# First projection of three batches moved into the first attention, in half units

## What is computed

```
qkv = x @ qkv_w.T                              # q, k, v of 16 heads
scores = alpha * tanh(q @ k.T / beta)
f, g: tanh(x @ [hex_w, q6_w].T), 12 values per token
scores += (f mixed by a 12x12 table per head) @ g.T
attn = softmax(causal(scores)); out = (attn @ v) @ out_w.T
```

## Time and profile before

| | |
|---|---|
| median of 3 runs | 4458.54 us (4456.73 to 4461.19) |
| the profiled execution's own time | 4471.63 us |
| span in its profile | 4469.8 us |
| busy share of the span | PE 86%, ACT 77%, DVE 64%, POOL 10% |
| mean granted clock of TensorE | 0.959 |
| tanh of layer 0's attention (L775), busy in all | 1102.9 us, 640 instructions |
| exp of layer 0's attention (L785) | 1065.6 us, 640 instructions |
| sums of layer 0's attention (L835) | 1569.5 us, 2560 instructions |

### The profile page before, as it was taken

The page is one execution under the profiler, slowest core; times in us unless marked ns, Lnnn a source line. Parts: engine busy times, 40 slices in busy tenths (PEclk is TensorE's granted clock), DMA queues, the critical chain, the costliest instruction groups (busy, mean ns, idle before and its releaser), DMA issues. The chain is left out here.

```text
span 4469.8 us, 66988 instructions
## 1 busy us (share of the span) xinstructions
PE 3854.6 (86%) x21966; PEld 1406.6 (31%) x21966; DVE 2840.0 (64%) x5324; ACT 3432.6 (77%) x3144; POOL 450.8 (10%) x407
## 2 busy tenths in 40 slices
PE   6958888888888888888888776758999999999787
PEld 2422222222222222222222463432222222222465
DVE  5637777777777777777777796872233332332588
ACT  2429999999999999999999412337999999999333
POOL 3520000000000000000000124650000000000133
PEclk9979999999999999999999888988999999999899
DMA  5851111112111112111111345562222222222332
GB/s 174 260 175 53 48 52 39 42 48 57 43 52 42 42 49 56 44 50 41 39 56 30 115 141 155 169 187 77 72 73 60 79 66 71 75 58 65 98 92 85
DMA packets 307816, 360.48 MB, mean 81 GB/s; under 512 B 56590, under 2 KB 237934, under 8 KB 307249
## 3 DMA queue, kind: packets, MB, share of 16 engines
q1 hardware_dynamic: 307508, 356.62, 27.4%
HBM read 228.15 MB, written 128.25 MB: 80 GB/s over the span
## 5 line engine op out<-in xcount | busy, mean ns | idle before, releaser
L835 DVE SCALAR_TENSOR_TENSOR att_prob<-att_tanh,alpha,ps 128x512 f32<-128x512 f32 (+3 forms) x2560 | 1569.5, 661 | 525.4 <-ACT att_tanh L775 333.9
L716 PE MATMUL ps<-att_q,att_k 99*128 99x512 bf16 (+7 forms) x5120 | 1196.7, 355 | 173.6 <-DMA att_v<-v_ones 79.1
L743 PE MATMUL ps<-att_prob,att_v 128*32 128x512 f32 (+3 forms) x10240 | 1215.1, 547 | 10.2 <-ACT att_prob L785 5.3
L775 ACT ACTIVATE att_tanh<-ps,rbeta 128x2048 f32<-128x2048 f32 (+3 forms) x640 | 1102.9, 1723 | 123.3 <-PE ps L716 123.3
L781 ACT ACTIVATE att_prob<-ps 128x1024 f32<-128x1024 f32 (+3 forms) x1280 | 1051.9, 920 | 78.4 <-PE ps L716 70.1
L785 ACT ACTIVATE att_prob<-att_prob 128x2048 f32<-128x2048 f32 (+3 forms) x640 | 1065.6, 1665 | 52.1 <-DVE att_prob L835 49.6
L725 PE MATMUL ps<-att_f,att_g 75*128 75x512 bf16 (+3 forms) x2560 | 854.0, 361 | 177.9 <-DVE att_prob L835 153.3
L716 PEld LDWEIGHTS ps<-att_q,att_k 96*128 96x128 bf16 (+1 forms) x5120 | 396.8, 99 | 1045.4 <-ACT att_prob L781 430.4
L823 DVE TENSOR_TENSOR att_prob<-att_prob,keep 128x256 f32<-128x256 f32 x512 | 211.5, 423 | 647.3 <-ACT att_prob L781 642.2
L725 PEld LDWEIGHTS ps<-att_f,att_g 75*128 75x128 bf16 x2560 | 235.7, 97 | 1060.8 <-DVE att_prob L835 1029.1
L743 PEld LDWEIGHTS ps<-att_prob,att_v 128*32 128x32 f32 x10240 | 202.5, 108 | 391.8 <-issue 147.2
(11 more groups left out here) (132 smaller groups left out, 2470.9 us busy)
## 6 DMA issues: line engine op xcount, KB each, us to landing
att_k<-k_parts SPq DMA_DIRECT2D x768, 64.0 KB
att_q<-q_parts SPq DMA_DIRECT2D x768, 64.0 KB
v_ones<-proj_vs SPq DMA_DIRECT2D x128, 256.0 KB, 3.1
att_v<-v_ones SPq DMA_DIRECT2D x128, 256.0 KB
post_o<-o_t SPq DMA_DIRECT2D x40, 512.0 KB, 5.1
att_f<-f_parts SPq DMA_DIRECT2D x384, 48.0 KB
o_t<-att_on SPq DMA_DIRECT2D x512, 32.0 KB, 1.9
q_parts<-proj_parts SPq DMA_DIRECT2D x32, 384.0 KB, 4.1
```

The source lines that it names most:

```text
L716: mm = pe.matmul(ps[:, bank, off:TG], keys, q_s[:, n % QU, h, off:TG], start=True, stop=True)
L743: mm = pe.matmul(ps[VW * h:VW * (h + 1), O0 + n % 2, off:TG], v_s[:, c % KU, kb % CB, h * VW:(h + 1) * VW], prob[:, S % R, h, off:TG], sta ...
L775: th.done(act.activation(tanh_s[:, S % 2, :, off:TG], ps[:, QK0:QK0 + HQ, off:TG], ACT.Tanh, scale=kn["rbeta"][:, 0:1]))
L835: sc.done(dve.scalar_tensor_tensor(prob[:, S % R, h, off:TG], tanh_s[:, S % 2, h, off:TG], kn["alpha"][:, 0:1], ps[:, E0 + h % 2, off:TG], ...
```

## The change

Layer 0's projection phase now handles batch 0 alone (`NB=1`). The projection of batches 1 to 3 (12 groups) is done inside the attention of the batch before it. A group has 9 units there: g, q0, q1, k0, k1, f0, f1, v0, v1; each unit but the two f is cut in two halves, so there are 16 halves per group, 64 per batch and 192 in all. One half is issued at the end of every second step of PE, in steps 2, 4, ... 128 of a batch's 160. Halves of g, q and k are one of the two 128-channel products of a tile; a half of v is one of two blocks of 128 tokens. The products gather in PSUM bank 7.

- That bank is taken from the outputs: `OU = 1`, so the first `weigh` of a group waits for the transpose of the group just before. This first `weigh` (the "late" one) is issued at the end of its PE step, behind `extra(S, 3)` and ahead of the half, in all 16 sets.
- DVE copies each finished unit except g out of PSUM (8 per group, 96 in all) between the second and third sum of the next step. `normalise` moves from there to the front of the step's sums.
- ACT makes g with one tanh of 12 x 512 per group, ahead of its exp.
- POOL, idle in attention until now, does the whole split: four operations per tile, 84 tiles.
- SP loads four weights and two groups of x behind the first of its loads, stores 7 tiles and 2 x 4 pieces of v per group and loads x further on, in turns with the attention's loads, five steps behind PE. The loads of a new batch wait until its projection is stored.
- `row_max_phase` gets the projection too, in its skipped body.

```
-    QK0, E0, O0 = 0, 4, 6
+    QK0, E0, O0, BG = 0, 4, 6, 7
+    OU = 1 if layer == 0 else 2
+    kinds = tiles + [("v", 0), ("v", 1)]
+    NU = len(kinds)
+    N_UNIT = (B - 1) * GB * NU if layer == 0 else 0
+    EVERY = 2
+    halves = [(gq * NU + u, half) for gq in range(GB) for u, (kind, _) in enumerate(kinds) for half in range(1 if kind == "f" else 2)]
+    def half_at(S):
+        b, s = divmod(S, NHQ * NST)
+        i, rest = divmod(s - 2, EVERY)
+        if not N_UNIT or b == B - 1 or rest or not 0 <= i < len(halves):
+            return None
+        return b * (GB * NU) + halves[i][0], halves[i][1]
...
         def _(sp):
...
+            def store_unit(j):
+                X, kind, m, tile, n = unit(j)
+                b, gq = X // GB + 1, X % GB
+                if kind == "v":
+                    bg_ev.wait(sp, j)
...
+                    if m == 1 and X + 2 < N_UNIT // NU:
+                        load_x(X + 2)
+                else:
+                    low.wait(sp, tile)
...
+                    parts_out.done(sp.dma_start(kn[f"{kind}_d"][:, row:row + n, :].rearrange("k r t -> r k t"), parts[0:n, tile % 2]), tile % 2)
...
+            for n in range(QU):
+                load(n)
+                if layer == 0 and n == 0:
+                    for name, t in (("wq", wq_s), ("wk", wk_s), ("wv", wv_s), ("w12", w12_s)):
+                        sp.dma_start(t[:], w[name]).then_inc(w_in, 16)
+                    load_x(0)
+                    load_x(1)
+            LATE = LAG + 3
+            for S in range(LATE, N + LATE):
...
+                if last:
+                    if n + QU < NG:
+                        o_tr.wait(sp, n)
+                        b = (n + QU) // (GB * NHQ)
+                        if layer == 0 and b > 0 and (n + QU) // GB % NHQ == 0:
+                            projected((b - 1) * GB + (n + QU) % GB)
+                        load(n + QU)
+                    store_o(n)
+                if unit_at(S - LATE) is not None:
+                    store_unit(unit_at(S - LATE))
...
         def _(pe):
+            def project(j, half):
+                X, kind, m, tile, n = unit(j)
+                if half == 0:
...
+                    bg_ev.wait(pe, j - 1)
+                if kind == "f":
+                    mm = pe.matmul(ps[0:n, BG], kn["Cq"][:].rearrange("p q e h -> p (q e h)")[:, m * n:(m + 1) * n], f12[:, X % 2], start=True, stop=True)
+                elif kind == "v":
+                    at_t = slice((2 * m + half) * P, (2 * m + half + 1) * P)
+                    for c in range(DC):
+                        mm = pe.matmul(ps[:, BG, half * D:(half + 1) * D], xt_s[:, X % 2, c, at_t], wv_s[:, c, :], start=c == 0, stop=c == DC - 1)
+                else:
+                    lhs = w12_s[:, half, :] if kind == "g" else (wq_s if kind == "q" else wk_s)[:, half, m * P:(m + 1) * P]
+                    mm = pe.matmul(ps[0:n, BG], lhs, xt_s[:, X % 2, half], start=half == 0, stop=half == 1)
+                if half == 1 or kind == "f":
+                    bg_ps.done(mm)
...
-                    o_tr.wait(pe, n - 2)
+                    o_tr.wait(pe, n - OU)
...
-                if S >= LAG:
+                late = layer == 0 and S >= LAG and at(S - LAG)[2] == 0
+                if S >= LAG and not late:
                     weigh(S - LAG)
...
                     extra(S, 3)
+                if layer == 0 and late:
+                    weigh(S - LAG)
+                if half_at(S):
+                    project(*half_at(S))
...
         def _(act):
+            def feature(j):
+                X, kind, m, tile, n = unit(j)
+                if kind == "g":
+                    bg_ps.wait(act, j)
...
+                    bg_ev.done(act.activation(f12[:, X % 2], ps[0:NF, BG], ACT.Tanh))
...
+                if S > 0 and unit_at(S - 1) is not None:
+                    feature(unit_at(S - 1))
                 if S > 0 and layer == 0:
...
         def _(dve):
+            if layer == 0:
+                dve.memset(vs[:], 1.0).then_inc(ones_set, 1)
...
+            def evict(j):
+                X, kind, m, tile, n = unit(j)
+                if kind == "v":
...
+                    bg_ev.done(dve.tensor_copy(vs[:, m, :, :, 0:HD], ps[:, BG].rearrange("p (t h d) -> p t h d", t=2, h=H)))
+                elif kind != "g":
+                    bg_ps.wait(dve, j)
+                    low.wait(dve, tile - 2)
+                    bg_ev.done(dve.tensor_copy(raw[0:n, tile % 2], ps[0:n, BG]))
...
-                        o_tr.done(dve.transpose(ot_s[:, v].rearrange("p b n -> p (b n)"), ps[:, O0 + v]))
+                        o_tr.done(dve.transpose(ot_s[:, v].rearrange("p b n -> p (b n)"), ps[:, O0 + G % OU]))
...
                 for h in range(HQ):
-                    if h == 2:
+                    if h == 0:
                         normalise(due, 2 if g <= 1 else 1)
+                    if h == 2 and S > 0 and unit_at(S - 1) is not None:
+                        evict(unit_at(S - 1))
...
+            @block.gpsimd
+            def _(pool):
...
+                    bg_ev.wait(pool, j)
+                    parts_out.wait(pool, u, tile // 2 - 1)
+                    hi.done(pool.tensor_copy(parts[0:n, u, 0], src))
...
+                    rest.done(pool.tensor_tensor(rem[0:n], src, parts[0:n, u, 0], ALU.subtract))
...
+                    mid.done(pool.tensor_copy(parts[0:n, u, 1], rem[0:n]))
...
+                    low.done(pool.tensor_tensor(parts[0:n, u, 2], rem[0:n], parts[0:n, u, 1], ALU.subtract))
...
-        project_phase(nc, kn, 0, {"wq": chunked(a["wq0"]), "wk": chunked(a["wk0"]), "wv": chunked(a["wv0"]), "w12": chunked(a["w12"]), "xt": chunked(a["x0_t"])}, None)
-        row_max_phase(nc, kn, 0)
-        attend_phase(nc, kn, 0)
+        project_phase(nc, kn, 0, w0, None, NB=1)
+        row_max_phase(nc, kn, 0, w0)
+        attend_phase(nc, kn, 0, w0)
```

More of the change, by code:

```diff
@@ L683, in _ @@
                 sp.dma_start(k_s[QROWS:QROWS + 3], kn["ones_d"][:, 0:KU * HQ * TG].rearrange("p (u h t) -> p u h t", u=KU, h=HQ)).then_inc(ones_in, 16)
[L684 to L694, removed]
+            for n in range(QU):
[7 more added lines that the diff above has]
+            for S in range(LATE, N + LATE):
+                it, g, *_, last = at(S - LATE)
+                n = it * GB + g
+                if last:
[8 more added lines that the diff above has]
+                    store_unit(unit_at(S - LATE))
             for u in range(2):
@@ L767, in _ @@
                 c.start(act)
+            def feature(j):
+                X, kind, m, tile, n = unit(j)
+                if kind == "g":
+                    bg_ps.wait(act, j)
+                    if X >= 2:
+                        low.wait(act, tile - 2 * NTL)
+                    bg_ev.done(act.activation(f12[:, X % 2], ps[0:NF, BG], ACT.Tanh))
             for S in range(N + 1):
@@ L848, in _, with row_max_phase @@
             assert not due
-def row_max_phase(nc, kn, layer):
+        if layer == 0:
+            @block.gpsimd
+            def _(pool):
+                for c in (hi, rest, mid, low):
+                    c.start(pool)
+                for j in range(N_UNIT):
+                    X, kind, m, tile, n = unit(j)
+                    if kind == "v":
+                        continue
+                    u = tile % 2
+                    src = f12[:, X % 2] if kind == "g" else raw[0:n, u]
+                    bg_ev.wait(pool, j)
+                    parts_out.wait(pool, u, tile // 2 - 1)
+                    hi.done(pool.tensor_copy(parts[0:n, u, 0], src))
+                    hi.wait(pool, tile)
+                    low.wait(pool, tile - 1)
+                    rest.done(pool.tensor_tensor(rem[0:n], src, parts[0:n, u, 0], ALU.subtract))
+                    rest.wait(pool, tile)
+                    mid.done(pool.tensor_copy(parts[0:n, u, 1], rem[0:n]))
+                    mid.wait(pool, tile)
+                    low.done(pool.tensor_tensor(parts[0:n, u, 2], rem[0:n], parts[0:n, u, 1], ALU.subtract))
+def row_max_phase(nc, kn, layer, w=None):
     SR, FR = QROWS, FROWS
@@ L885, in _ @@
             with sp.If(wide == 1):
+                if layer == 0:
+                    for name, t in (("wq", wq_s), ("wk", wk_s), ("w12", w12_s)):
+                        sp.dma_start(t[:], w[name]).then_inc(w_in, 16)
+                    with sp.Fori(0, B - 1) as b:
+                        for gq in range(GB):
+                            J0 = b * NTB + gq * NTL
+                            wait(sp, split, J0 * 4 + 1, ph.passed)
+                            sp.dma_start(xt_s[:], w["xt"][:, :, bass.ds((b + 1) * T + gq * TG, TG)]).then_inc(x_in, 16)
+                            for t, (kind, m) in enumerate(tiles):
+                                n, per = rows_of[kind], {"g": NF, "f": H * NF}.get(kind, D)
+                                row = (b + 1) * (GB * per) + gq * per + m * n
+                                wait(sp, split, (J0 + t) * 4 + 5, ph.passed)
```

(6 more changed lines are left out.)

104 lines of the change are left out of this document (100 added, 4 removed).

## The result

The changed kernel takes 4560.27 us (median of 4 runs, 4557.7 to 4562.05) against 4458.06 for the kernel before: a ratio of 1.0228, 95% interval 1.021 to 1.0246. I had forecast 4414 and a range from 4340 to 4475.

A forecast was written before the change was run, and what follows sets the result against it. Attention was taken as bound by ACT (94% busy), PE close behind. Removing projection groups gives -173.0, added attention and start costs +129: net -44 on 4471.6, 4427.6, less 13.1 for the median: 4414 us, range 4340 to 4475.

The forecast's parts named there:

- The removed phase: First projection: twelve of its groups go, at 14.42 us each, saving 173.0 us.
- The start: Kernel start: six more DMA issues ahead of the second load cost +3 us; bounds 0 and +7.
- Plain full steps: Full steps without late weigh or copy: PE's half fits the slack and is free, steps staying at 3.65 us.
- The copy: DVE's copy of a finished unit in full steps: takes 0.69 us, 0.39 us lost per copy.
- The diagonal steps: Halves at r0 and r2: the pair costs 1.51 of its 1.86 us; nine pairs, 13.6 us per batch.
- A late step with a half at full clock: Full step with late weigh and half: next tanh 0.86 us late, 1.1 on average with copies; ten per batch, 11 us.
- The other signs: Changed profile: tanh's waits for q-k products up 80 us or more, exp's waits for the sums up 20 to 35.
- I keep the clock as it was in the sum: Whole attention sum: granted clock taken as unchanged, though halves might keep it up and lower the sum.
- the tanh keeps its time: Full steps with late weigh but no half (batch 3): q-k products at 826.38, so no loss.
- set starts: Late weigh in step 0 costs about 1.0 us per set, 2.1 with halves in steps 0 and 2; 7.9 per batch.
- a rival of the fast side: Denser work in r0, r2 and step 6 or 14 keeps the clock up: -20 us, 4394; chance 0.12.
- The third rival: PE and DVE delay each other, ACT waits in every step: +86 us, 4544; chance of any slower outcome 0.15.

The follow-up runs named there:

- the fill over 128 channels: Kernel before with late weigh, one output bank and normalise ahead of the sums, no projection, plus four useless 128-channel products in the weigh's old place: 4452.3 us.
- the fill over 12 channels: Kernel before with late weigh, one output bank, normalise ahead of the sums, no projection, plus four useless 12-channel products in the weigh's old place: 4555.4 us.
- the first two runs: Kernel before with the late weigh alone: 4571.6 us; the same plus one output bank and normalise ahead of the sums: 4538.3 us.
- the moved copy: Changed kernel with only DVE's copy of a finished unit moved ahead of the step's first sum: 4488.6 us, ratio 1.0062.
- the run with everything together and the copy ahead of the sums: Changed kernel with late steps' half in the weigh's old place, batch 3 with two banks, no half in r2, copy before the first sum: 4348.5 us.

## Why the prediction was wrong

**The removed phase**: forecast 173.0, measured 173.8. **The start**: the wait before the second group's first tanh is 8.24 us instead of 5.07, +3.2 against +3. **Plain full steps**: 3.65 to 3.67 with a half and no copy, as worked out. **The copy**: 0.684 us long, forecast 0.69:

```profile
L934 DVE COPY att_raw<-ps x72: 678/684/686, 188.0 to 1882.9; 128x512 f32<-128x512 f32 x48, 96x512 f32<-96x512 f32 x24
```

and 0.5 lost per copy against 0.39; all plain and other steps together lost 29.6 against some 22 (3 x 7.5). **The diagonal steps**: in the nine sets with halves in all three groups' ends the pairs cost 2.3, 1.7 and 1.7, mean 1.9 against 1.51; that is the whole of a pair's 1.86, so the part that I took as hidden was not hidden, and in all they cost some 11 us more than forecast. **A late step with a half at full clock**: in the first set step 7 escaped the fall (clock 1.00) and took 4.67 us against 3.67, so +1.00; forecast 0.86. **The other signs**: the exp's waits for the sums rose from 49.6 to 78.3 us, inside the 20 to 35 more that I named; the tanh's for the q-k products by 207, where I had named 80 or more.

**The step that failed** is the one sentence "I keep the clock as it was in the sum", and with it the working by which, without a half, "the tanh keeps its time" behind a late weigh. Late steps and set starts were to cost 61 us in all (ten late full steps at 1.1 and 7.9 for the set starts per batch, 4 in batch 3), part of that in diagonal steps; the late steps alone cost 155.8 + 20.7 = 176.5. That difference, some 115 to 120 us, is nearly all of the attention's excess of 134 over the forecast of 129; the diagonal pairs are most of the rest. Where the clock held, the arithmetic of the queue was not far off (0.14 us in the step above; a set's start at full clock, the sixth set's, cost 0.87 + 1.68 = 2.55 against 2.1), but it held at 4 of 64 places.

I had the row that warned: the clock fell behind a diagonal stretch in which PE waited. I read it as a fixed cost that more work could only lessen, and so made its removal a rival of the fast side, though I wrote there that a half beyond the fall would cost double. But the change does not only add work: the late weigh takes 1.0 us of fp32 work out of the third step behind the diagonal, where PE has just run the narrow weighs of r2 and r3 and where the clock of the kernel before already fell at 14 of 64 places, and piles it into the next. The rule of the Trainium skill (TensorE: Matmul & The Clock Gate, on the HAM clock gate), that activity releases the throttle, agrees with the fill over 128 channels (58 places without it, 8 with it), but not if activity is read as the profile's busy time, since the fill over 12 channels left 60. I had applied it to the sum of PE's work and not to its order in time.

The third rival gave 4544, near the result, by luck: it had ACT wait in every step, whereas plain steps keep 3.65. Its exposed price per half (252 / 192 = 1.31) is even near the mean loss in batches 0 to 2 (245.5 / 192 = 1.28), but two thirds of that stand behind the 48 late weighs.

Left open: why a few late places keep the clock (the same code falls in one set and not in another), how much of the 33 us between the first two runs belongs to `normalise` and how much to the bank, and how the 72 us of the moved copy divide between copy and clock.

## What to carry to other kernels

When an instruction group is moved on TensorE, look at what stays in the place it leaves, not only at what it lands behind: a step that becomes light can drop the clock from 2.4 to 1.2 GHz, and what is queued next then costs up to twice as much. Where a light place can't be avoided, put independent work of full height into it (here the projection's own halves: 131 us for the order of two lines), and keep products over few channels out of it. And price a copy on an in-order engine by what stands behind it: the same 0.68 us cost 0.5 between the sums and about 0.15 ahead of them.

## What the runs showed of the hardware that I had not expected

- A stretch in which the profile shows PE busy with fp32 products over 12 channels did not keep the clock (60 of 64 places down), the same products over 128 channels did (8 of 64), at equal durations of 612 and 617 ns.
- Useless work made the kernel faster: 4538.3 to 4452.3 us.
- DVE's product with two SBUF operands, 424 ns in the middle and 427 at most in the kernel before, took up to 1148 beside POOL's split in the changed one:

```profile
L952 DVE TENSOR_TENSOR att_oq<-att_ot,att_rc x128: 416/424/1148, 176.7 to 4243.3; 128x256 f32<-128x256 f32 x128
```

The median did not move, so it costs little here. 12 of the 128 stood beside one of POOL's subtractions (TENSOR_TENSOR, two SBUF operands); 11 of them took 702 to 1148 ns, and each of these ended 0.28 us behind POOL's instruction, as if it could not proceed until that was done. The twelfth had begun together with POOL's and took 419. The Trainium skill (GPSIMD Engine Reference, Specifications) says that GpSimd shares its SBUF interfaces with VectorE and that DVE instructions with two SBUF inputs contend; the trace agrees. The copy out of PSUM, which stays at 678 to 686, is no such instruction, but only one of them stood beside a subtraction of POOL; in the run with everything together and the copy ahead of the sums it was five, and no copy took over 693.
